# Softmax sums in a decoder layer: from matmuls of ones to exponentials of the row scores, and the transposed mask by a GpSimd selection

## The chip, the cores and the metric

One core of a Trainium2 chip runs one launch of the whole kernel. The metric is the device time of that launch in microseconds (us). The engines are TensorE (PE in the profile, its weight loads PEld), VectorE (DVE), ScalarE (ACT), GpSimd (POOL) and SyncE (SP). All five run their own instruction lists in order and wait for each other on semaphores.

## What is computed

Four batches of 512 tokens of width 512 pass through one decoder layer: attention with 16 heads of width 32 that share one key and one value head, a second block that is a quantised two-product network, and a gated feed-forward of width 1376 with low-rank experts. Only the attention is touched by the change.

```python
qkv = einsum('bsd,ed->bse', x, Wqkv_w) + Wqkv_b           # q: 16 heads x 32, k: 32, v: 32
scores = einsum('bqhd,bkd->bhqk', q, k) * HEAD_DIM ** -0.5
scores = where(tril(ones(S, S)), scores, finfo.min)
attn = softmax(scores, axis=-1)
ctx = einsum('bhqk,bkd->bqhd', attn, v)
out = einsum('bsd,ed->bse', ctx, out_w) + out_b
x = x + out                                              # of layernorm(x)
# then x = x + xattn(layernorm(x), ...), x = x + ffn(layernorm(x), ...)
```

## The kernel before

**Work.** Every engine's list is made from one list of steps, `ORDER`. It is merged from four streams: A (attention, `attention_steps`), L (layer norms and the quantised block, `layer_steps`), F (feed-forward, `feed_forward_steps`) and W (splitting the weights into a high and a low part, `preparation_steps`). Strings of the letters A, L, F and W (`FIRST`, `SECOND`, twice `STEADY`, `LAST`) say from which stream the next step is taken. Batches overlap: while batch b is in feed-forward, batch b+1 is in the quantised block and batch b+2 in attention. Batches 0 and 1 have no feed-forward beside their attention; batches 2 and 3 each have the whole feed-forward of an earlier batch beside theirs (110 of its gate and up pieces lie between the last `out` step of batch 1 and that of batch 2, and 110 more up to that of batch 3). After batch 3's attention only L and F are left.

**Attention.** A batch is done in four groups g of four heads. A group first needs the largest score of each query row. Step `max` (six per group, `MAX_GROUPS`; lines 1007 and 1011 on PE, 1295 on DVE) writes masked scores, rows = queries, into a PSUM slot, and DVE reduces them to `negm`, minus the largest score. Step `rows` turns `negm` with a PE transpose (L1018), splits it into high and low parts (ACT L800, DVE L1301), and two DMAs put them as extra rows under the queries in `qst`. Step `scores` (four per group, one for each tile kt of 128 keys; two halves each) writes transposed scores (rows = keys) less the row's largest score: two bf16 matmuls of `mask_bf` (L1029) put the mask into the diagonal tile, two matmuls (L1031) add the scores. ACT takes the exponential into `probs` (L811). Step `values` (L1045) multiplies `probs` with `v` into the PSUM tile `av` and with `ones` into the PSUM tile `den`, four heads side by side in four column groups of the array. Step `sums` copies `av` (DVE L1310) and `den` (ACT L818), step `context` takes the reciprocal of 128x512 sums in two halves (DVE L1315) and multiplies (DVE L1318), `split_context` splits the result (ACT L823, POOL L707), and `out` multiplies with the output weights.

**Buffers.** Two PSUM slots of two banks are shared by `turn1`, `kv`, `q`, `v`, `max`, `rows`, `scores`, `out` and the quantised block. A step claims the next of the two in turn (`Tenants.claim`), and PE waits there until the engine that read the slot last is done: for `max` that is DVE's reduction (`s_max`), for `scores` ACT's exponential (`p_ready`). The feed-forward and W use two other tiles, `ring`.

**Order on ACT.** ACT also does the tanh of each gate tile (L905), the split of `hd` (L909), and issues the DMA that loads the next `gu` tile.

## Time and profile before

| | |
|---|---|
| median of 3 runs | 1017.0 us (1016.59 to 1024.69) |
| profiled execution, its own time | 1015.68 us |
| its span | 1013.9 us |
| mean granted TensorE clock | 0.943 |
| PE busy | 923.5 us (91%) |
| DVE busy | 616.7 us (61%) |
| ACT busy | 313.1 us (31%) |
| POOL busy | 248.5 us (25%) |

Busy time of PE counts the pipelined latency of every matmul, so a busy PE can still be short of its rate. What one matmul takes from the next one is better read from the chain of work that ended last, where a piece runs only to the start of the next.

### The profile page before, as it was taken

The numbers are of one execution on the slowest core, as the hardware profiler recorded it, in microseconds if no ns is written. First come the engines' busy times: TensorE is split into PE (matmuls) and PEld (weight loads), VectorE is DVE, ScalarE is ACT, GpSimd is POOL, SyncE is SP. The second block draws the span as 40 slices with busy tenths as digits, with TensorE's granted clock in tenths as the row PEclk, the third lists the DMA queues.
The fourth block names the chain that finished last, engine by engine and source line by source line (L and its number), as shares of the span: only waits on it lengthen the run. The fifth ranks groups of instructions, "written<-read, shape, count | busy, mean of one in ns | idle before, by whom it ended". The sixth has DMA issues, their size and how long they took to land.

```text
span 1013.9 us, 13146 instructions
## 1 busy us (share of the span) xinstructions
PE 923.5 (91%) x5206; PEld 654.6 (65%) x5214; DVE 616.7 (61%) x865; ACT 313.1 (31%) x496; POOL 248.5 (25%) x217
## 2 busy tenths in 40 slices
PE   2898899587999999999999999999979999779997
PEld 1664456454457776667577776666757787568785
DVE  2345768778687687767565886765477565332222
ACT  2323442244353215342423135333222431121110
POOL 3612322421543022123210131231204033011110
PEclk9857979688799999999999999999999999999999
DMA  8963651832666843348344733354335455525442
GB/s 277 312 189 116 233 216 24 246 128 88 238 197 253 202 172 123 126 171 340 116 154 93 230 123 104 147 226 141 107 140 199 152 185 209 205 94 206 161 170 89
DMA packets 42913, 174.98 MB, mean 173 GB/s; under 512 B 5404, under 2 KB 8220, under 8 KB 32868
## 3 DMA queue, kind: packets, MB, share of 16 engines
q1 hardware_dynamic: 36804, 119.09, 34.7%
q10 hardware_dynamic: 6048, 55.05, 14.9%
q8 instruction: 42, 0.69, 0.3%
q14 instruction: 19, 0.16, 0.0%
HBM read 127.52 MB, written 33.75 MB: 159 GB/s over the span
## 4 chain that ended last, share of the span: by engine, by line
PE 74%; DVE 13%; issue 4%; DMA 3%; SPq 3%; ACT 2%; POOL 1%; POOLq 0%; DVEq 0%; ACTq 0%
PE ring L935 12%; PE ring L937 11%; PE ring L936 11%; PE av L1045 4%; PE slot L1031 4%; DVE negm L1295 4%; PE ring L1177 3%; PE den L1045 3%; PE slot L1011 3%; SPq L573 3%; PE slot L935 3%; PE slot L936 2%; PE slot L937 2%; PE slot L1114 2%; PE slot L1029 2%
## 5 line engine op out<-in xcount | busy, mean ns | idle before, releaser
L734 POOL TENSOR_TENSOR hd_l<-hd,hd_h 128x512 fp32r<-128x512 f32 x44 | 57.7, 1312 | 401.2 <-ACT hd_h L909 401.2
L935 PE MATMUL ring<-xT_h,gu 128*128 128x512 f32 x352 | 145.6, 414 | 5.0 <-DVE gated L1502 2.9
L936 PE MATMUL ring<-xT_l,gu 128*128 128x512 f32 x352 | 138.4, 393 | 0.0
L937 PE MATMUL ring<-xT_h,gu 128*128 128x512 f32 x352 | 138.3, 393 | 0.0
L1295 DVE TENSOR_REDUCE negm<-slot 128x4 f32<-128x512 f32 (+2 forms) x96 | 98.6, 1043 | 59.6 <-PE slot L1011 59.0
L811 ACT ACTIVATE probs<-slot 128x256 f32<-128x256 f32 (+3 forms) x128 | 85.0, 700 | 89.8 <-PE slot L1031 89.8
L935 PEld LDWEIGHTS ring<-xT_h,gu 128*128 128x128 f32 x352 | 66.8, 190 | 29.4 <-issue 11.5
L937 PEld LDWEIGHTS ring<-xT_h,gu 128*128 128x128 f32 x352 | 66.6, 189 | 14.9
L1541 DVE TENSOR_TENSOR total<-ring,total 128x512 f32<-128x512 f32 x64 | 44.0, 688 | 51.0 <-PE ring L937 50.9
L1031 PE MATMUL slot<-qst,kst 98*128 98x128 f32 (+3 forms) x256 | 74.8, 387 | 0.0
L936 PEld LDWEIGHTS ring<-xT_l,gu 128*128 128x128 f32 x352 | 67.0, 190 | 11.6
L1011 PE MATMUL slot<-kst,qst 96*128 96x128 f32 (+3 forms) x256 | 73.4, 397 | 0.0
L935 PE MATMUL ring<-dn,hd_h 128*128 128x512 f32 x176 | 70.1, 398 | 0.2 <-DVE ad_sum L1521 0.2
L937 PE MATMUL ring<-dn,hd_l 128*128 128x512 f32 x176 | 69.2, 393 | 0.0
L936 PE MATMUL ring<-dn,hd_h 128*128 128x512 f32 x176 | 69.1, 393 | 0.0
L909 ACT ACTIVATE hd_h<-hd 128x512 fp32r<-128x512 f32 x44 | 27.8, 631 | 119.1 <-DVE hd L1513 119.1
L905 ACT ACTIVATE gated<-ring 128x512 f32<-128x512 f32 x44 | 26.3, 599 | 122.5 <-PE ring L1177 122.3
L1513 DVE SCALAR_TENSOR_TENSOR hd<-gated,ring 128x512 f32<-128x512 f32 x44 | 30.2, 687 | 51.7 <-PE ring L1177 36.1
L1502 DVE SCALAR_TENSOR_TENSOR gated<-gated,ring 128x512 f32<-128x512 f32 x44 | 29.9, 680 | 50.5 <-ACT gated L905 50.5
L1315 DVE RECIPROCAL rden<-rden 128x256 f32<-128x256 f32 x32 | 55.8, 1744 | 0.1
L1029 PE MATMUL slot<-mask_bf 128*128 128x128 bf16 x256 | 38.8, 236 | 16.9 <-DVE negm L1295 7.7
L1045 PE MATMUL av<-probs,v 128*32 128x512 f32 (+3 forms) x512 | 52.3, 484 | 1.3 <-DVE cx L1310 1.1
(194 smaller groups left out, 1754.2 us busy)
## 6 DMA issues: line engine op xcount, KB each, us to landing
gu<-gu_parts ACTq DMA_DIRECT2D x42, 1280.0 KB, 5.5
dn<-dn_parts SPq DMA_DIRECT2D x12, 1728.0 KB, 7.7
gu_parts<-gu SPq DMA_DIRECT2D x11, 1280.0 KB, 5.7
qst<-qT_h SPq DMA_DIRECT2D x64, 128.0 KB, 2.4
raw_gu<-gu SPq DMA_DIRECT2D x11, 640.0 KB, 7.3
dn_parts<-dn SPq DMA_DIRECT2D x11, 576.0 KB, 7.7
dn<-dn_parts SPq DMA_DIRECT2D x4, 1152.0 KB, 5.1
x_in<-x SPq DMA_DIRECT2D x8, 512.0 KB, 4.8
```

Of the source, the lines that this page charges most:

```text
L734: pool.tensor_tensor(hd_l[:, i, :], hd[:, i, :], hd_h[:, i, :].bitcast(F32), ALU.subtract).then_inc(hd_lo.sem, 1)
L811: act.activation(probs[:, 2 * (step % 2) + pr, :, 0:n], slots[SLOT["scores", b, step, pr]][:, :, 0:n], ACT.Exp, scale=SCALE).then_inc(p_re ...
L935: pe.matmul(out_, w_hi_, m_hi_, start=start, stop=False, skip_group_check=True)
L936: pe.matmul(out_, w_hi_, m_lo_, start=False, stop=False, skip_group_check=True)
L937: return pe.matmul(out_, w_lo_, m_hi_, start=False, stop=stop, skip_group_check=True)
L1011: mm = pe.matmul(ps[:, bank, at * n:(at + 1) * n], qst[0:KROWS, 4 * g + h0 + h, qt * P:(qt + 1) * P], kst[0:KROWS, 0:n], start=False, stop ...
L1029: pe.matmul(ps[:, j, 0:P], mask_bf[:, 0, :], mask_bf[:, 2, :], start=True, stop=False, skip_group_check=True)
L1031: mm = pe.matmul(ps[:, j, 0:n], kst[0:KROWS + 2, kt * P:(kt + 1) * P], qst[0:KROWS + 2, 4 * g + 2 * pr + j, kt * P:T], start=False, stop=T ...
L1045: mm = pe.matmul(to[HD * c:HD * c + HD, kt * P:T], weights, probs[:, 2 * (step % 2) + c // 2, c % 2, 0:n], start=(kt == TT - 1), stop=(kt ...
L1295: dve.tensor_reduce(negm[:, h0:h0 + heads, qt].rearrange("p (a c) -> p a c", a=2), slots[SLOT["max", b, g, i]][:, :, 0:heads // 2 * n].rea ...
L1315: dve.reciprocal(rden[:, cols], rden[:, cols]).then_inc(rden_ready.sem, 1)
L1541: dve.tensor_tensor(total[:, tt, :], ring[RING["down", b, s, tt]][:, :], total[:, tt, :], ALU.add)\
```

## The change

The row sums no longer come from products with `ones`. Behind DVE's reduction of a `max` slot a new step `weigh` lets ACT take the exponential of each head's part of that slot (in place, bias = `negm`), with the sum along the row as a second output into `row_sum`. The slot is now free when these are done (`s_sum`). A new step `inverse` takes the reciprocal of 16 sums per row (DVE), which travel in the same transpose as the next group's `negm` (`rows`, five per batch instead of four), are split into high and low parts, and are spread over 32 rows per head by four matmuls (`spread`, with a loaded 0/1 matrix `spread_w`) into the PSUM tile `inv` in place of `den`. ACT copies it to `inv_sb`. `context` is one DVE multiplication of `av` in PSUM with `inv_sb`, per half. The mask of the transposed scores is no longer added by matmuls: POOL's `affine_select` sets the masked part of the diagonal tile of `probs` to zero behind ACT's exponential. A `scores` slot is free at the exponential (`p_exp`); `values` waits for the selection (`p_ready`). The scale 32^-0.5 moves from the exponential into the keys, with one more ACT copy of them. The `dn` tile has 3 slots instead of 4. The four strings of letters become one, `TURNS`, written out for all steps, with three `fill` steps (4, 1 and 4 spare matmuls of 256 columns).

```diff
@@ attention_steps
     for i in range(MG):
         yield ("max", b, 0, i)
+        yield ("weigh", b, 0, i)
...
-        yield ("scores", b, step)
+        yield ("scores", b, step, 0)
+        yield ("scores", b, step, 1)
...
-            for which in range(2):
-                yield ("values", b, step - 1, which)
+            yield ("values", b, step - 1)
         for key in maxima_among(g, idx):
             yield ("max", b, *key)
-        if idx == 0 and g:
-            yield ("sums", b, g - 1)
+            yield ("weigh", b, *key)
...
+        if idx == 3:
+            yield ("spread", b, g)
@@
-FIRST = (
...
+TURNS = (
+    "AAAAAAAAWAAAAWAAAAWWAAAAWAWAWAAWAAAAAAAAWAAAWAAAAAAAAAAWA4WAAAAWAAWWAAAAAWAAAAAAAWWAAAAAAAAAAAAAAAAAAAAAAAWAAA"
...
@@ gpsimd
+            def scores(b, step, pr):
+                diagonal = probs[:, 2 * (step % 2) + pr, :, 0:P]
+                pool.wait_ge(p_exp.sem, p_exp.at(b, 2 * step + pr + 1))
+                pool.affine_select(diagonal, diagonal, [[0, 2], [1, P]], ALU.is_ge, 0.0, base=0,
+                                   channel_multiplier=-1).then_inc(p_ready.sem, 1)
@@ scalar
+            def weigh(b, g, i):
+                qt, h0, heads = MAX_GROUPS[i]
+                n, per_bank = (qt + 1) * P, heads // 2
+                ps = slots[SLOT["max", b, g, i]]
+                act.wait_ge(s_max.sem, s_max.at(b, MG * g + i + 1))
+                for h in range(heads):
+                    part = ps[:, h // per_bank, h % per_bank * n:(h % per_bank + 1) * n]
+                    at = (h0 + h) * TT + qt
+                    ins = act.activation(part, part, ACT.Exp, bias=negm[:, g, at:at + 1], accum_out=row_sum[:, g, at:at + 1])
+                ins.then_inc(s_sum.sem, 1)
...
-                act.activation(rden[:, :], den[:, :], ACT.Copy).then_inc(den_out.sem, 1)
+                act.activation(inv_sb[:, :], inv[:, :], ACT.Copy).then_inc(inv_out.sem, 1)
@@ tensor
-                ps = in_slots.claim(pe, ("max", b, g, i), s_max, s_max.at(b, MG * g + i + 1))
+                ps = in_slots.claim(pe, ("max", b, g, i), s_sum, s_sum.at(b, MG * g + i + 1))
...
-                    for j in range(2):
-                        pe.matmul(ps[:, j, 0:P], mask_bf[:, 0, :], mask_bf[:, 2, :], start=True, stop=False, skip_group_check=True)
...
-                to, weights, read = ((av, v[:, kt, :], av_out), (den, ones[:, :], den_out))[which]
...
+            def spread(b, g):
+                pe.wait_ge(inv_lo.sem, inv_lo.at(b, g + 1))
...
+                for tt in range(TT):
+                    mm = pe.matmul(inv[:, tt * P:(tt + 1) * P], spread_w[:, tt, :], rows_hl[:, g, :], start=True, stop=True,
+                                   skip_group_check=True)
@@ vector
+            def inverse(b, g):
+                dve.wait_ge(s_sum.sem, s_sum.at(b, MG * g + MG))
+                dve.reciprocal(negm[:, g + 1, HD:HD + 4 * TT], row_sum[:, g, :]).then_inc(inv_ready.sem, 1)
...
-                dve.reciprocal(rden[:, cols], rden[:, cols]).then_inc(rden_ready.sem, 1)
...
-                dve.tensor_tensor(cx[:, g % 2, cols], cx[:, g % 2, cols], rden[:, cols], ALU.mult).then_inc(cx_ready.sem, 1)
+                dve.tensor_tensor(cx[:, g % 2, cols], av[:, cols], inv_sb[:, cols], ALU.mult).then_inc(cx_ready.sem, 1)
```

How this stands in the engines' lists. On PE, in batch 0's first group of heads, before (L1045 values and sums, L1018 the turn of `negm`, L1029 mask and L1031 scores):

```order
L1045 MATMUL av<-probs,v 32x128 x4
L1045 MATMUL den<-probs,ones 32x128 x4
L1018 MATMUL slot<-cst,negm 16x128
L1029 MATMUL slot<-mask_bf 128x128 x2
L1031 MATMUL slot<-qst,kst 128x384 x2
L1029 MATMUL slot<-mask_bf 128x128 x2
L1031 MATMUL slot<-qst,kst 128x384 x2
L1045 MATMUL av<-probs,v 32x256 x4
L1045 MATMUL den<-probs,ones 32x256 x4
```

The products with `ones` and the mask matmuls are gone, the turn is three times as wide, and pieces of W (`fold`, L997 and L1003) stand in between. The same place in the changed kernel (L1097 values, L1075 the turn, L1084 scores):

```order
L1097 MATMUL av<-probs,v 32x128 x4
L1075 MATMUL slot<-cst,negm 48x128
L997 MATMUL ring<-fold 128x128 x8
L1084 MATMUL slot<-qst,kst 128x384 x4
L1003 MATMUL ring<-fold 128x512
L1097 MATMUL av<-probs,v 32x256 x4
```

On ACT, from the first weight tile that is split in batch 0 up to the first exponentials, before:

```order
L767 ACTIVATE gu_102<-raw_gu_108 128x1280
L773 ACTIVATE dn<-raw_dn_110 128x576
L800 ACTIVATE negm_hl<-slot 16x128
L767 ACTIVATE gu_103<-raw_gu_109 128x1280
L811 ACTIVATE probs<-slot 128x2x128 x2
```

In the changed kernel the exponentials of the row scores (L835) stand between these, two or four behind each reduction:

```order
L835 ACTIVATE slot,row_sum<-slot,negm 128x128 x4
L799 ACTIVATE dn<-raw_dn_114 128x576
L835 ACTIVATE slot,row_sum<-slot,negm 128x256 x4
L793 ACTIVATE gu_107<-raw_gu_113 128x1280
L835 ACTIVATE slot,row_sum<-slot,negm 128x384 x2
L799 ACTIVATE dn<-raw_dn_115 128x576
L835 ACTIVATE slot,row_sum<-slot,negm 128x384 x2
L835 ACTIVATE slot,row_sum<-slot,negm 128x512 x4
L844 ACTIVATE rows_hl<-slot 16x128
```

Each of these now stands between the reduction and the next claim of that slot. On DVE, at the end of batch 0's attention, before:

```order
L1310 COPY cx<-av 128x512
L1315 RECIPROCAL rden<-rden 128x256
L1318 TENSOR_TENSOR cx<-cx,rden 128x256
L1315 RECIPROCAL rden<-rden 128x256
L1318 TENSOR_TENSOR cx<-cx,rden 128x256
```

The copy and the two wide reciprocals are gone there; a reciprocal of 16 columns and a split of the turned rows come in:

```order
L1360 RECIPROCAL negm<-row_sum 128x16
L1369 TENSOR_TENSOR rows_hl<-slot,rows_hl 16x128
L1380 TENSOR_TENSOR cx<-av,inv_sb 128x256 x2
```

In both orders the last `out` steps of the four batches have 0, 0, 110 and 220 gate and up pieces, and all 11 weight tiles of W by batch 1, ahead of them.

## Rows read from the trace of the kernel before

**Rows 1.** The page: span, granted clock in 40 slices (tenths), the reduction's group.

```profile
span 1013.9 us, 13146 instructions
...
PEclk9857979688799999999999999999999999999999
...
L1295 DVE TENSOR_REDUCE negm<-slot 128x4 f32<-128x512 f32 (+2 forms) x96 | 98.6, 1043 | 59.6 <-PE slot L1011 59.0
```

**Rows 2.** Six stretches: busy us (instructions) of five engines, granted clock, DMA.

```profile
0.00:41.00 41.00, 21.63 (x96) 16.30 (x96) 11.47 (x20) 14.27 (x23) 16.85 (x24) 1.00 0.88 296
41.00:152.00 111.00, 96.19 (x616) 56.30 (x617) 63.87 (x79) 38.21 (x59) 33.03 (x28) 0.75 0.58 198
152.00:312.00 160.00, 133.93 (x858) 84.42 (x859) 124.70 (x164) 62.84 (x96) 59.25 (x48) 0.84 0.50 162
312.00:524.00 212.00, 209.05 (x1246) 149.38 (x1247) 146.53 (x207) 70.34 (x114) 46.54 (x41) 1.00 0.51 177
524.00:737.00 213.00, 210.22 (x1254) 150.27 (x1255) 142.21 (x196) 70.92 (x115) 45.30 (x39) 1.00 0.44 151
737.00:1013.00 276.00, 252.49 (x1143) 197.90 (x1143) 127.93 (x202) 56.54 (x90) 47.55 (x38) 0.98 0.45 164
```

**Rows 3.** The residual addition behind `out`: the whole run, then 300 to 350 us.

```profile
L1323 DVE TENSOR_TENSOR x<-slot,x x8: 1208/1225/1226, 152.0 to 737.2; 128x1024 f32<-128x1024 f32 x8
...
L1323 DVE TENSOR_TENSOR x<-slot,x x2: 1208/1216/1225, 308.0 to 311.8; 128x1024 f32<-128x1024 f32 x2
```

**Rows 4.** The chain that ended last, shares of 41 to 312 us.

```profile
by line: DVE negm L1295 12.0%; PE av L1045 7.7%; PE slot L1011 6.6%; PE slot L1031 6.4%; PE den L1045 6.3%; DVE rden L1315 4.5%; PE ring L951 4.3%; PE ring L945 4.0%; issue 3.8%; PE slot L1007 3.6%; PE slot L1029 3.3%; SPq L573 3.1%; PE slo
```

**Rows 5.** The same chain, shares of 312 to 737 us.

```profile
by line: PE ring L935 14.9%; PE ring L937 13.4%; PE ring L936 13.3%; PE slot L1031 5.4%; PE av L1045 5.0%; PE den L1045 4.2%; PE ring L1177 3.8%; SPq L573 3.6%; PE slot L1011 3.5%; PE slot L937 3.4%; PE slot L935 3.4%; PE slot L936 3.4%; PE
```

**Rows 6.** Pieces of the chain, 485 to 500 us: start, us, what.

```profile
485.13 0.65 PE den L1045 x8
...
489.02 0.86 PE den L1045 x8
490.77 0.13 PE slot L1029 x2
...
491.97 0.22 PE den L1045 x8
...
497.25 0.43 PE den L1045 x8
```

**Rows 7.** Pieces of the chain, 640 to 652 us.

```profile
640.37 0.11 PE slot L1018
...
645.68 0.40 PE slot L1011 x4
```

**Rows 8.** ScalarE's groups by form: busy us, mean ns, idle before.

```profile
L811 ACT ACTIVATE probs<-slot 128x1024 f32<-128x1024 f32 x32 | 31.3, 1020 | 27.5 <-PE slot L1031 27.5
...
L811 ACT ACTIVATE probs<-slot 128x256 f32<-128x256 f32 x32 | 11.7, 383 | 19.2 <-PE slot L1031 19.2
L794 ACT ACTIVATE qT_h<-slot,bq_sb 128x512 fp32r<-128x512 f32 x16 | 11.0, 688 | 26.0 <-PE slot L937 25.7
...
L885 ACT ACTIVATE prob<-ring 128x32 f32<-128x32 f32 x4 | 0.8, 198 | 2.5 <-PE ring L1152 2.4
```

**Rows 9.** VectorE's wide reciprocals, by form.

```profile
L1315 DVE RECIPROCAL rden<-rden 128x256 f32<-128x256 f32 x32 | 55.8, 1744 | 0.1
```

**Rows 10.** The multiplication behind them: least, median and greatest ns.

```profile
L1318 DVE TENSOR_TENSOR cx<-cx,rden x32: 424/426/2857, 94.5 to 724.1; 128x256 f32<-128x256 f32 x32
```

**Rows 11.** GpSimd's groups by form nearest to a selection.

```profile
L707 POOL TENSOR_TENSOR hT_l<-cx,hT_h 128x256 fp32r<-128x256 f32 x32 | 25.3, 789 | 92.2 <-ACT hT_h L823 92.2
...
L644 POOL MEMSET kst<- 32x512 f32 x1 | 0.5, 520 | 0.1
```

**Rows 12.** TensorE's longest wait, 312 to 737 us: total, times, longest.

```profile
PE ring L935 <- DVE gated L1502: 2.9, 2, 1.6
```

**Rows 13.** Line 1045, what its engine stood idle for: us, times.

```profile
ACT probs L811: 8.8, 25
```

More of the change, by code:

```diff
@@ L143, in attention_steps @@
                 yield (("ln1_stats", "ln1_norm")[step - LN1_STEP], 1, h)
-    for which in range(2):
-        yield ("values", b, 15, which)
-    yield ("sums", b, 3)
+    yield ("values", b, 15)
     for hf in range(2):
@@ L287, in tenants_of @@
             slots.append(step)
-        elif name == "scores":
-            slots += [(*step, pr) for pr in range(2)]
         elif name == "prep_gu":
@@ L796, in rows_ @@
             def rows_(b, g):
+                ps = slots[SLOT["rows", b, g]]
                 act.wait_ge(m_ps.sem, m_ps.at(b, g + 1))
[L798 to L812 removed]
```

281 lines of the change are left out of this document (160 added, 121 removed).

## The prediction

> **What bounds the kernel now.** I read the busy times and clock by stretch first, then the chain of work that ended last in each, then the waits. The run falls into three parts, cut at the last residual addition of batches 1 and 3, at 312 and 737 us [rows 3]. From 312 to 737 us, where batches 2 and 3 have a feed-forward beside their attention, TensorE (PE) is busy 419 of 425 us at the full 2.4 GHz [rows 2], and its longest wait is 2.9 us in all [rows 12]: what PE is relieved of there comes back as time. From 41 to 312 us, the attention of batches 0 and 1, nothing is full: PE 230 and VectorE (DVE) 189 of 271 us, with a granted clock of 0.75 and 0.84 [rows 2]. The chain there changes between DVE's reductions (12.0%), PE and the reciprocals (4.5%) [rows 4], so this part is a latency problem, in which a longer way through a PSUM slot counts. After 737 us there is no attention, and the change doesn't reach it.
>
> **PE from 312 to 737 us.** This holds 8 groups of four heads. The products with ones take 0.22, 0.43, 0.65 and 0.86 us for the four key tiles [rows 6], 2.16 us a group, 17.3 us for 8; the chain's 4.2% of 425 us, 17.9, says the same [rows 5]. The mask takes 0.13 us for two matmuls [rows 6], 64 times, 8.3 us. Added are the spreading matmuls, four of 128 columns with 128-column weights a group, nearest to the four of 0.40 us in [rows 7]: 8 x 0.40 = 3.2 us; and one more turn a batch at 0.11 us [rows 7], 0.2 us. Net: -25.6 + 3.4 = **-22 us**. As 110 gate and up pieces stay in each of the two stretches, nothing fills the room but what was there. The cover that this needs: ScalarE (ACT), which is busy 141 of 425 us [rows 2], must do its new work beside PE.
>
> **What ACT gets.** An exponential costs 383 ns for 256 columns and 1020 for 1024, 0.83 ns a column; a 512-column activation with a per-row bias costs 688 ns [rows 8]. So the heads' parts of 128, 256, 384 and 512 columns cost 0.37, 0.48, 0.58 and 0.69 us, four of each a group: 8.5 us, or 1.41 us behind each of the six reductions, and 135 us in 16 groups. No row shows what the second output, the row sum, costs. Lower end nothing; upper end one further short instruction each, by the shortest ACT row 198 ns [rows 8], 51 us in 256. I take nothing, as it would be 0.2 us behind a head at most, and keep the 51 us for the range. On this the Trainium skill ("VectorE: DVE Perf Modes", Two Vector instructions with no wait between them) says that an operation which writes out its accumulator is two instructions. That is said of VectorE, and no row here shows it of ScalarE; if it held, 0.8 us more would stand behind a reduction of four heads, and it speaks against this change. The copy of `den` is replaced by a copy of the same size; a third key copy, about 0.7 us a batch, hides behind PE's query products.
>
> **41 to 312 us, removed.** From the chain: products with ones 6.3% of 271 us, 17.1 us; mask 3.3%, 8.9 us; reciprocals 4.5%, 12.2 us [rows 4]. In all DVE loses 55.8 us of reciprocals in the run [rows 9] for 16 tiny ones. The 26 us of PE I count in full, since PE is also what is late next there. Of the 12 us of DVE I count half: behind a reciprocal DVE has layer norms and weight folds waiting. Together -32 us.
>
> **41 to 312 us, added.** (1) The slot. The reductions hold 12.0% of the chain, 32.5 us, so with 1.04 us each [rows 1] 31 of the 48 lie on it. PE's part of such a slot is about 0.6 us (lines 1007 and 1011, 10.2% of 271 us [rows 4], over 48). Before, one slot could be filled while the other was reduced, and DVE set the pace, 1.04 us. Now a slot is held for 0.6 + 1.04 + 1.41 = 3.05 us, and two of them give 1.53 us: 0.49 us more, 31 times, 15 us. Ends: 0 if other steps always fill the gap, 44 us (31 x 1.41) if the exponentials are never overlapped. I take 15, because both slots exist and the interleaved steps are as many as before. Queued behind PE's wait for a slot are the scores and values of the group before; behind ACT's exponentials, the exponentials of `probs`. (2) The selection on GpSimd (POOL), 128 x (2 x 128), which no row shows. Nearest are 789 ns for a two-input operation on 128x256 and 520 ns for a memset of 512 columns, half of which is 260 [rows 11]; I take 0.5 us, one input and one output. PE stands behind an exponential at line 1045 only 25 times [rows 13]; 25 x 0.5 is 12 us, and as `values` comes after the next step's `scores`, I take a third, 4 us (ends 0 and 20). A gain isn't possible: it only adds to a way. POOL itself has room, 92 of 271 us busy plus 32 [rows 2]. (3) Spreading, 8 x 0.40 us, some at half clock: 4 us. (4) First batch: the load of the spread matrix, two bias and matrix copies: 1 us. Together +24, so **-8 us** net, from -38 to +35 by the ends.
>
> **Contention.** The multiplication of the context, two inputs in SBUF, is 426 ns in the median and 2857 at most [rows 10]; its new form reads `av` from PSUM. The Trainium skill ("GPSIMD Engine Reference", Key points) says that GpSimd shares its SBUF interfaces with VectorE, with contention on two SBUF inputs; the 2857 ns would be of that kind. It would make 128 more GpSimd instructions cost DVE something, and the new multiplication gain. I count neither.
>
> **Sum.** -22 - 8 = -30 us on the profiled 1015.7 us, which is 1.3 us below the median of 1017.0. Against the median: **987 us**. The nine spare matmuls, 3 slots of `dn` for 4, and the rewritten order count nothing: the former stand where PE waits, the middle one is touched by three stores.
>
> **Rivals.**
> *Slots and ACT's queue decide (slower), 1035 us.* In the full stretch the tanh of a gate tile stands in ACT's queue behind two to four exponentials (1.4 us or more), and `up`'s products cover it only for a short time: PE already waits 2.9 us for `gated` [rows 12]. Half a us more on each of 22 column tiles is 11 us; a third of the 48 maxima finding its slot 1.41 us late is 22 us. That makes -22 + 33 = +11 there. With 30 us instead of 15 for the slot, the latency part is at -8 + 15 = +7: 1017 + 18 = 1035. It decides from the point where ACT's way through a slot is longer than what PE has between two claims of it. For it: PE runs in order and has just two slots. Against: ACT is a third busy there. 10%.
> *Nothing net in the latency part, or lost again, 1003 us.* The slot costs 23 us or more; only the -22 stays, with some of it given back. 15%.
> *A colder clock, 1001 us.* The clock of 0.75 and 0.84 means 56 and 51 us at 1.2 GHz [rows 2]. PE is given less to do between the same waits, and may hold the low level for longer. 50 us more of it, with PE on half of the chain, is 50 x 0.5 x 0.5 = 13 us. The Trainium skill ("TensorE: Matmul & The Clock Gate", Why this matters for your kernels) says that gaps without PE work bring the half clock back. The page of the profile shows the low slices just where PE has gaps [rows 1]. 5%.
> *No change, 1012 us.* The mask and the ones turn out to have been cover for waits (transfers of `gu` among them), and the full stretch gives only half. 10%.
> *All of it, 966 us.* The exponentials hide, and the 38 us come back whole: -22 - 38 + 9. 18%.
>
> **Numbers.** The forecast, 975 to 1000, has 42%. A measurement of this kernel tells about 1% from no change, 1007 to 1027 us. Faster by more: 42 + 18 + 15 + 5, less a little of the 1003 case that passes 1007, 0.78; same 0.12; slower 0.10. The range of 8 in 10 leaves out the slower case, the upper part of no change and the lowest of the best case: 958 to 1014.
>
> **What the next profile would show.** Right: no matmuls with ones, PE busy down by some 80 us in its pipelined count, ACT up to about 450 us, 312-to-737's counterpart near 403 us with PE still above 97% busy; first two batches 41 to about 304. Row sums: a second ACT instruction behind each exponential, or none. Wrong: PE waits at line 1058 for `s_sum` or at a gate for `gated` of more than 10 us in the stretch of batches 2 and 3; a selection of over 1 us; a mean clock under 0.93.

## The result

The changed kernel takes **1040.2 us** in the median (1038.06 to 1043.18, four runs), and the kernel before, run beside it, 1020.3 us (1016.59 to 1024.69). The ratio is 1.0207, 95% interval 1.0173 to 1.0242: about 2% slower, where 987 us, 3% faster, was forecast. The time lies above the forecast's range. Medians are of all runs, ratios of the fast runs alone, which leaves out one slow run each in two of the experiments.

The page of the changed kernel, first its span, then the granted clock in 40 slices, then the reduction's group, the one of [rows 1]:

```profile
span 1041.4 us, 12384 instructions
...
PEclk9855558755668999999999999999998999989999
...
L1354 DVE TENSOR_REDUCE negm<-slot 128x4 f32<-128x512 f32 (+2 forms) x96 | 100.3, 1045 | 91.4 <-PE slot L1062 91.0
```

The middle four of the six stretches of [rows 2] have these counterparts. Columns are the stretch, its length, busy us (instructions) of PE, PEld, DVE, ACT and POOL, granted clock, DMA share and GB/s:

```profile
41.00:174.00 133.00, 116.50 (x474) 70.11 (x475) 49.48 (x76) 72.98 (x191) 49.10 (x63) 0.56 0.54 184
174.00:354.00 180.00, 144.10 (x695) 91.95 (x696) 115.02 (x173) 99.91 (x232) 68.58 (x77) 0.69 0.44 149
354.00:554.00 200.00, 193.49 (x1040) 142.32 (x1041) 125.55 (x188) 104.02 (x243) 60.84 (x73) 0.99 0.51 178
554.00:767.00 213.00, 201.93 (x1086) 149.22 (x1087) 132.16 (x196) 106.81 (x250) 58.98 (x71) 0.99 0.46 156
```

They are cut at the last residual addition of each batch, as before [rows 3]. Those of the changed kernel start at 173.8, 353.5, 553.9 and 766.2 us. So, counted from 41 us, batches 0 and 1 take 312.5 us instead of 270.8, **41.7 more**, batches 2 and 3 412.7 instead of 425.4, **12.7 less**, and the rest 275.2 instead of 276.7. The clock fell in the first two from 0.75 and 0.84 [rows 2] to 0.56 and 0.69: 229 of 312 us at 1.2 GHz, where it had been 106 of 271.

Such stretch figures come from one profiled run of each kernel. That of the changed kernel took 1043.2 us, 3.0 above its median, and that of the kernel before 1015.7, 4.6 below the median beside it, at one of its highest clocks (0.943, where its runs beside the experiments had 0.926 to 0.943). So 7.6 of the 27.5 us between the two profiles are scatter. In batches 0 and 1, where the clock varies, I take differences under some 5 us as not shown; in batches 2 and 3 the figures repeat within 1 us among the kernels that hardly differ there (412.7, 412.3 and 412.1 us).

One correction to this cut. The new order does one batch's routing and low-rank entry earlier, ahead of batch 1's last `out`. TensorE's groups of the changed kernel, 41 to 354 us (busy us, mean ns), hold it; in those of the kernel before, 41 to 312 us, these products don't occur:

```profile
L1205 PE MATMUL ring<-xT_h,route_hl 128*16 128x512 f32 x4 | 1.6, 395 | 0.0
L1206 PE MATMUL ring<-xT_l,route_hl 128*8 128x512 f32 x4 | 1.6, 393 | 0.0
L987 PE MATMUL ring<-xT_h,gaua_h 128*128 128x512 f32 x4 | 1.6, 393 | 0.0
L988 PE MATMUL ring<-xT_l,gaua_h 128*128 128x512 f32 x4 | 1.6, 390 | 0.0
L989 PE MATMUL ring<-xT_h,gaua_l 128*128 128x512 f32 x4 | 1.6, 390 | 0.0
L1214 PE MATMUL ring<-tail_c,lT 16*128 16x8 f32 x8 | 1.1, 254 | 0.0
```

That is 9.1 us of busy time moved, not lost. If each of them counts as a microsecond of the run in both places, batches 0 and 1 lose 32.6 us and batches 2 and 3 gain **3.6**, where -8 and -22 were forecast. (In batches 2 and 3 TensorE is busy nearly all the time, so there this holds; in batches 0 and 1 it is an upper bound.)

ScalarE's groups by form. The new exponentials take 127.6 us in all, and behind each stands a second instruction that reads the row sum out:

```profile
L835 ACT ACTIVATION_READ_ACCUMULATOR slot<-slot,negm 128x1 f32 x256 | 51.4, 201 | 0.0
L835 ACT ACTIVATE slot<-slot,negm 128x512 f32<-128x512 f32 x64 | 42.0, 657 | 21.4 <-DVE negm L1354 21.4
L835 ACT ACTIVATE slot<-slot,negm 128x384 f32<-128x384 f32 x64 | 35.3, 552 | 31.9 <-DVE negm L1354 31.8
...
L835 ACT ACTIVATE slot<-slot,negm 128x256 f32<-128x256 f32 x64 | 28.6, 447 | 11.0 <-DVE negm L1354 10.9
...
L835 ACT ACTIVATE slot<-slot,negm 128x128 f32<-128x128 f32 x64 | 21.7, 339 | 39.5 <-DVE negm L1354 39.5
```

What TensorE waited for in batches 0 and 1 (us, times, longest), then in batches 2 and 3. The waits behind L835 are those of its slots:

```profile
PE slot L1084 <- ACT slot L835: 14.2, 13, 2.0
PE slot L1058 <- ACT slot L835: 13.5, 12, 2.3
PE slot L1058 <- DMA qst<-qT_h: 8.2, 2, 4.2
PE slot L1084 <- DVE rows_hl L1369: 5.2, 5, 3.8
...
PE slot L1075 <- ACT slot L835: 2.2, 1, 2.2
...
PE slot L1140 <- ACT slot L835: 1.6, 1, 1.6
```

```profile
PE ring L987 <- DMA gu<-gu_parts: 6.3, 3, 3.9
PE slot L1058 <- issue: 3.4, 2, 2.1
PE ring L987 <- DVE y_u L1592: 2.1, 2, 1.1
```

In the first two batches 31.5 us in 27 waits stand behind the exponentials. Before, 22 waits there stood behind the reductions alone, 16.7 us. The waits are less than half of the loss: in the profiles TensorE's idle time grew there from 41 us (270.8 less 230.0 busy) to 52 (312.5 less 260.1), and its busy time, with fewer products to do, from 230 to 260 us, 9 of them the moved routing. In batches 2 and 3 no wait at all stands behind the exponentials. The waits for `gu` have grown there from 1.0 us to 6.3; [rows 12] had 2.9 us, for `gated`, as the longest, and no such wait is left.

### The profile page after: what moved, and what is told of

Same layout as the page of the kernel before. It is cut to its first block, busy times and chain, and to the rows that moved or that the text cites. A ratio compares the mean times of both kernels' runs of the same rounds, so it can differ in the third digit from the quotient of the medians.

```text
span 1041.4 us, 12384 instructions
## 1 busy us (share of the span) xinstructions
PE 928.3 (89%) x4515; PEld 666.5 (64%) x4523; DVE 559.5 (54%) x849; ACT 455.2 (44%) x1030; POOL 301.9 (29%) x346
## 3 DMA queue, kind: packets, MB, share of 16 engines
q10 hardware_dynamic: 6048, 55.05, 14.9%
## 4 chain that ended last, share of the span: by engine, by line
PE 73%; DVE 9%; ACT 5%; issue 5%; DMA 4%; POOL 2%; SPq 1%; POOLq 0%; DVEq 0%; ACTq 0%
PE ring L987 11%; PE ring L988 10%; PE ring L989 10%; PE slot L1084 5%; PE av L1097 5%; PE slot L1062 4%; PE ring L1239 4%; DMA gu<-gu_parts 3%; PE slot L987 3%; PE slot L989 3%; PE slot L988 3%; PE ring L997 2%; ACT slot L835 2%; DVE negm L1354 2%; PE slot L1176 2%
## 5 line engine op out<-in xcount | busy, mean ns | idle before, releaser
L835 ACT ACTIVATE slot<-slot,negm 128x128 f32<-128x128 f32 (+3 forms) x256 | 127.6, 499 | 103.8 <-DVE negm L1354 103.5
L1354 DVE TENSOR_REDUCE negm<-slot 128x4 f32<-128x512 f32 (+2 forms) x96 | 100.3, 1045 | 91.4 <-PE slot L1062 91.0
L862 ACT ACTIVATE probs<-slot 128x256 f32<-128x256 f32 (+3 forms) x128 | 87.5, 703 | 57.4 <-PE slot L1084 56.3
L727 POOL TENSOR_SCALAR_AFFINE_SELECT probs<-probs 128x256 f32<-128x256 f32 x128 | 59.8, 474 | 159.9 <-ACT probs L862 159.2
L1084 PE MATMUL slot<-qst,kst 98*128 98x128 f32 (+3 forms) x256 | 79.8, 415 | 21.0 <-ACT slot L835 14.2
L1062 PE MATMUL slot<-kst,qst 96*128 96x128 f32 (+3 forms) x256 | 83.2, 438 | 0.0
L1084 PEld LDWEIGHTS slot<-qst,kst 98*128 98x128 f32 x256 | 52.8, 239 | 46.2 <-ACT slot L835 21.2
L1058 PE MATMUL slot<-mask_bf 128*128 128x128 bf16 (+1 forms) x192 | 38.0, 290 | 25.9 <-ACT slot L835 13.5
```

Of the source, the lines that this page charges most:

```text
L727: pool.affine_select(diagonal, diagonal, [[0, 2], [1, P]], ALU.is_ge, 0.0, base=0, channel_multiplier=-1).then_inc(p_ready.sem, 1)
L835: ins = act.activation(part, part, ACT.Exp, bias=negm[:, g, at:at + 1], accum_out=row_sum[:, g, at:at + 1])
L862: act.activation(probs[:, 2 * (step % 2) + pr, :, 0:n], slots[SLOT["scores", b, step, pr]][:, :, 0:n], ACT.Exp)\
L1062: mm = pe.matmul(ps[:, bank, at * n:(at + 1) * n], qst[0:KROWS, 4 * g + h0 + h, qt * P:(qt + 1) * P], kst[0:KROWS, 0:n], start=False, stop ...
L1084: mm = pe.matmul(ps[:, j, 0:n], kst[0:KROWS + 2, kt * P:(kt + 1) * P], qst[0:KROWS + 2, 4 * g + 2 * pr + j, kt * P:T], start=True, stop=Tr ...
L1354: dve.tensor_reduce(negm[:, g, 0:4 * TT].rearrange("p (h q) -> p h q", q=TT)[:, h0:h0 + heads, qt].rearrange("p (a c) -> p a c", a=2), slo ...
```

## The experiments

Each was timed beside the kernel before; "stretch" figures are batches 0 and 1, then batches 2 and 3, of the profiled run, against 270.8 and 425.4 us of the kernel before and 312.5 and 412.7 us of the changed one. Cold is the time at 1.2 GHz within batches 0 and 1 (106 us before, 229 after).

**The products put back.** First the mask as a product (here with no effect on the scores, as it is overwritten):

```diff
+                    pe.matmul(ps[:, j, 0:P], mask_bf[:, 0, :], mask_bf[:, 1, :], start=True, stop=True, skip_group_check=True)
                 for j in range(2):
```

> The changed kernel with the 256 bf16 mask products back on TensorE, two ahead of each half of a scores step, overwritten by the scores (the result is unchanged). Clock theory (the products taken away had kept TensorE above what it needs for 2.4 GHz): the time at 1.2 GHz in the first two batches, 229 us of 41 to 354 us, falls by 40 us or more and the run is at 1030 us or less although 8 us of work are added in each half of the run. Slot theory (the exponentials in the max slots make the loss): the clock hardly moves and the run is 8 to 17 us longer than the changed kernel, 1048 to 1057 us.

Measured: 1047.3 us, 1.0274 (1.0225 to 1.0323); stretches 313.2 and 417.2. The products cost nothing in the first two batches and 4.5 us in the full ones. Cold fell from 229 to 201 us, less than the clock theory asked, and brought no time.

Then also four products a step in place of those with `ones`, into `inv`:

```diff
+                if 4 * b + g + (kt == 0):
+                    pe.wait_ge(inv_out.sem, 4 * b + g + (kt == 0))
+                for c in range(4):
+                    mm = pe.matmul(inv[HD * c:HD * c + HD, kt * P:T], v[:, kt, :], probs[...], start=True, stop=True, ...)
                 mm.then_inc(pv_done.sem, 1)
```

> The changed kernel with the mask products and the second set of products with probs back (into the inv tile, overwritten by the spreading products), so that TensorE has the same work as in the kernel before plus spreading. Clock theory: time at 1.2 GHz near the 106 us of the kernel before, run at 1020 to 1030 us. Slot theory: batches 2 and 3 give back their 12 us and more, nothing is gained ahead of them, run at 1065 to 1085 us.

Measured: 1076.4 us, 1.0566 (1.0514 to 1.0617); stretches 328.5 and 431.6. All the products are worth 36 us, 18.9 of them in the full stretch and 16.0 in batches 0 and 1. So they do cost something there, a third of the 47.8 us that they kept TensorE busy in the kernel before; with them cold falls from 229 to 198 us. The wait that comes with them, for ScalarE's copy of `inv`, held nothing up: TensorE's matmuls never stood behind it, a weight load once for 0.6 us.

**The exponentials of the row scores left out**, one short ScalarE instruction behind each reduction in their place:

```diff
-                for h in range(heads):
-                    ...
-                    ins = act.activation(part, part, ACT.Exp, bias=negm[:, g, at:at + 1], accum_out=row_sum[:, g, at:at + 1])
+                ins = act.activation(row_sum[...][:, heads_of, qt], negm[...][:, heads_of, qt], ACT.Exp, scale=0.0)
                 ins.then_inc(s_sum.sem, 1)
```

> The changed kernel without the exponentials of the row scores: one short ScalarE instruction per max step writes ones in place of the sums, so the softmax is not normalised. Slot theory: the max slots are free 1.2 to 2.2 us earlier, 48 times in the first two batches, run at 1000 us or less, and TensorE's waits for ScalarE at max and scores slots (27.7 us) go. Clock theory alone: the waits go, but the clock stays at 0.5 to 0.6 in the first two batches, run at 1020 to 1035 us.

Measured: 1013.8 us, 0.9941 (0.991 to 0.9972); stretches 285.1 and 411.3. The exponentials cost 26 us by the medians; by stretches 27.4 us in batches 0 and 1, where cold falls to 177 us without them, and 1.4 in batches 2 and 3. The run isn't at the 1000 us or less of the slot theory. Without the exponentials (41 to 326 us), then with them (41 to 354 us), columns as in the stretches above:

```profile
41.00:326.00 285.00, 247.35 (x1167) 155.78 (x1169) 162.00 (x249) 113.75 (x217) 119.37 (x141) 0.69 0.53 182
...
41.00:354.00 313.00, 260.60 (x1166) 162.06 (x1169) 164.49 (x248) 172.89 (x423) 117.69 (x140) 0.63 0.48 164
```

So of the 28 us that lie between these two lines about 15 are idle time of TensorE (52.4 for 37.7), and 13 are products that take longer. In batches 2 and 3 TensorE waits as before for `gu`, and so not because of the exponentials:

```profile
PE ring L986 <- DMA gu<-gu_parts: 8.0, 3, 3.7
PE slot L1057 <- issue: 3.4, 2, 2.1
PE ring L986 <- DVE y_u L1591: 2.1, 2, 1.0
```

**The order of the kernel before**, with all else as changed:

```diff
-TURNS = (...)
+FIRST = (...)   # the four strings and the attention steps of before;
+                # weigh behind its max, both score halves together, spread and inverse behind their step
```

> The changed kernel with the order of the kernel before: its letters, each old attention step replaced by the new steps up to its counterpart, no spare matmuls. Order theory (the rewritten order makes the loss): 1005 to 1020 us. Slot and clock theory: within 10 us of the changed kernel's 1040 us, since the work and the slots are the same.

Measured: 1071.0 us, 1.0505 (1.0453 to 1.0558); stretches 319.6 and 430.8. The new order gains 31 us. In the old one TensorE stands 15 us behind the exponentials in batches 2 and 3, and never for `gu`.

**Spare products for the clock**: two more of 256 columns ahead of each `max` and `scores` in batches 0 and 1, with the exponentials and without them.

```diff
             for name, *where in ORDER:
+                if name in ("max", "scores") and where[0] < 2:
+                    fill(2)
```

> The changed kernel with two spare bf16 products of 256 columns on TensorE ahead of each max and scores step of batches 0 and 1 (112 places, 24 us of work at 2.4 GHz, 48 us at 1.2 GHz), written to the free ring tile, where they run while TensorE would wait for a slot. Clock theory (the time at 1.2 GHz, 229 us of 41 to 354, costs some 40 us there): the time at 1.2 GHz falls by more than 80 us and the run is at 1030 us or less despite the added work. Slot theory alone: the spare products are only work, 1050 to 1070 us.

> The same spare products in the kernel without the row exponentials (1014 us; its softmax is not normalised). Clock theory: time at 1.2 GHz from 177 us to under 100 us, run at 1000 us or less. Otherwise 1020 to 1035 us.

Measured: 1039.3 us, 1.0193 (1.0166 to 1.0221), stretches 305.0 and 417.0; and 1018.1 us, 0.9981 (0.9954 to 1.0007), stretches 284.1 and 409.9. Cold falls from 229 us to 150, and without the exponentials from 177 to 119; the clock of the page, with both exponentials and spare products, is now

```profile
PEclk9856889757679989999999999999999999899999
```

and the time stays, or with the exponentials left out grows by 4 us, the intervals overlapping (1040.2 and 1013.8 us without the spare products). What the clock gives, the spare work takes.

**The kernel before without the removed products**, all else as it was: neither mask nor `ones` products (but for one group), so masking and sums are left out:

```diff
-                    for j in range(2):
-                        pe.matmul(ps[:, j, 0:P], mask_bf[:, 0, :], mask_bf[:, 2, :], ...)
...
-                for c in range(4):
+                for c in range(4) if which == 0 or b + g == 0 else ():
```

> The kernel before, in its own order, without the mask products and, but for the first group of heads, without the products with ones (the mask and the sums are wrong); ScalarE and VectorE do all that they did. It asks what TensorE's relief is worth alone. If all of it comes back: 1020 - 26 (batches 2 and 3) - 25 (batches 0 and 1) = 967 to 975 us. If the clock takes the part of batches 0 and 1 back, 990 to 1000 us with more than 140 us at 1.2 GHz ahead of 312 us.

Measured: 997.2 us, 0.9752 (0.9697 to 0.9808); stretches 271.7 and 401.2. This is the experiment that decides on my sum. In the full stretch the products are worth 24.2 us (25.6 forecast). In batches 0 and 1 the profiles show nothing for them, and the interval (20 to 31 us in all) leaves at most some 7 us outside of batches 2 and 3; 26 had been counted. TensorE's groups of the same products there, in this kernel,

```profile
L1029 PE MATMUL slot<-qst,kst 98*128 98x128 f32 (+3 forms) x128 | 46.7, 479 | 18.7 <-DVE negm L1293 8.1 <-DVE negm_hl L1299 6.7 <-ACT probs L811 1.5
L1011 PE MATMUL slot<-kst,qst 96*128 96x128 f32 (+3 forms) x128 | 44.9, 470 | 0.0
L1043 PE MATMUL av<-probs,v 128*32 128x128 f32 (+3 forms) x256 | 33.8, 615 | 1.8 <-DVE cx L1308 1.7
L945 PE MATMUL ring<-fold 8*128 8x128 f32 x160 | 23.8, 359 | 0.0
...
L951 PE MATMUL ring<-fold 8*128 8x512 f32 x22 | 18.3, 923 | 0.6 <-DVE raw_gu L1230 0.6
```

in the kernel before, 41 to 312 us, with the removed `den` and mask (L1029) among them,

```profile
L1011 PE MATMUL slot<-kst,qst 96*128 96x128 f32 (+3 forms) x128 | 41.8, 444 | 0.0
L1031 PE MATMUL slot<-qst,kst 98*128 98x128 f32 (+3 forms) x128 | 41.6, 417 | 0.0
L1045 PE MATMUL av<-probs,v 128*32 128x128 f32 (+3 forms) x256 | 28.5, 525 | 1.3 <-DVE cx L1310 1.1
L1045 PE MATMUL den<-probs,ones 128*32 128x128 f32 (+3 forms) x256 | 27.3, 504 | 0.0
L1029 PE MATMUL slot<-mask_bf 128*128 128x128 bf16 x128 | 20.5, 248 | 16.9 <-DVE negm L1295 7.7 <-DVE negm_hl L1301 6.9 <-DVE hid L1436 1.1
L945 PE MATMUL ring<-fold 8*128 8x128 f32 x160 | 20.0, 314 | 0.0
...
L951 PE MATMUL ring<-fold 8*128 8x512 f32 x22 | 16.3, 828 | 0.5 <-DVE raw_gu L1232 0.5
```

and in the changed kernel:

```profile
L1062 PE MATMUL slot<-kst,qst 96*128 96x128 f32 (+3 forms) x128 | 50.7, 521 | 0.0
L1084 PE MATMUL slot<-qst,kst 98*128 98x128 f32 (+3 forms) x128 | 49.8, 505 | 20.5 <-ACT slot L835 14.2 <-DVE rows_hl L1369 5.2 <-DVE hid L1498 1.1
L1097 PE MATMUL av<-probs,v 128*32 128x128 f32 (+3 forms) x256 | 35.5, 643 | 0.0
L997 PE MATMUL ring<-fold 8*128 8x128 f32 x160 | 28.2, 406 | 0.0
...
L1003 PE MATMUL ring<-fold 8*128 8x512 f32 x22 | 21.8, 1091 | 0.0
```

The same five groups (scores, maxima, `av` and the two of the weight folds) take 148.2 us before, 167.5 without the removed products and 186.0 in the changed kernel. 47.8 us of busy time go (27.3 `den`, 20.5 mask), and the rest grows, by 19.3 us in the one and 37.8 in the other, since more of it runs at 1.2 GHz (160 us and 229, for 106).

**The selection left out** (the diagonal tiles stay unmasked):

```diff
-                pool.affine_select(diagonal, diagonal, [[0, 2], [1, P]], ALU.is_ge, 0.0, ...).then_inc(p_ready.sem, 1)
...
-                pe.wait_ge(p_ready.sem, ...)
+                pe.wait_ge(p_exp.sem, ...)
```

> The changed kernel without the GpSimd selection: values wait for the exponential itself, the mask of the transposed scores is missing. If the selection lies on the way, as VectorE and TensorE never wait for it by name (1.8 us of waits), 1035 to 1040 us; if it costs what the prediction had counted, 4 us, 1036; if the selection carries the loss, 1025 us or less.

Measured: 1040.3 us, 1.0195 (1.0142 to 1.0247); stretches 311.9 and 412.1. It costs nothing. Its duration in the changed kernel, least, median and greatest:

```profile
L727 POOL TENSOR_SCALAR_AFFINE_SELECT probs<-probs x128: 398/409/1397, 72.8 to 748.9; 128x256 f32<-128x256 f32 x128
```

**The exponentials alone, added to the kernel before** (sums still from `ones`, order as before):

```diff
+            def weigh(b, g, i): ...      # as in the change
-                ps = in_slots.claim(pe, ("max", b, g, i), s_max, ...)
+                ps = in_slots.claim(pe, ("max", b, g, i), s_sum, ...)
```

> The kernel before, in its own order, with the row exponentials and their sums added behind every reduction and the max slots held until they are done (the sums are not used; all products stay). Slot theory: the first two batches take some 27 us longer as between the changed kernel and its form without exponentials, or more, since this order was not laid out for it: 1045 to 1075 us. If the exponentials cost only beside the freed products, 1020 to 1030 us.

Measured: 1090.8 us, 1.0703 (1.0665 to 1.0742); stretches 325.1 and 444.6: 54.3 and 19.2 us more. TensorE waited 48.8 us behind them in batches 0 and 1, and 14.9 in 2 and 3, by all its waits at a slot.

**The way of the sums left out as well as the exponentials**: no `inverse`, no wide turn, no `spread`; the context is multiplied by 0.5.

```diff
-                dve.tensor_tensor(cx[:, g % 2, cols], av[:, cols], inv_sb[:, cols], ALU.mult)
+                dve.tensor_scalar(cx[:, g % 2, cols], av[:, cols], 0.5, None, ALU.mult)
```

> The changed kernel without the row exponentials and without all that carries the sums (reciprocal, the wider turn, its two splits, spreading products, copy of inv; the context is multiplied by 0.5, the softmax is not normalised). Left of the change: fewer products, selection, the new order. If the way of the sums adds waits of its own (rows of the next group wait for the sums of this one), the first two batches fall from 285 us to 270 or less and the run is at 995 us or less. If only the clock and the order matter there, 1008 to 1014 us.

Measured: 1008.9 us, 0.9888 (0.986 to 0.9916): 5 us less than with it; stretches 288.8 and 406.1. The gain lies in batches 2 and 3 (5.2 us), and the first two are far from the 270 us that waits of this way's own would have given back.

**The selection alone, in the kernel before.** Only the mask products go, sums and order stay:

```diff
-                        pe.matmul(ps[:, j, 0:P], mask_bf[:, 0, :], mask_bf[:, 2, :], ...)
...
+            def scores(b, step):
+                for pr in range(2):
+                    ...
+                    pool.affine_select(diagonal, diagonal, [[0, 2], [1, P]], ALU.is_ge, 0.0, ...)
```

> The kernel before, in its own order, with only the second part of the change: the mask by GpSimd's selection in place of 256 mask products. If batches 2 and 3 give back the 8 us of their 64 pairs of products and the clock takes the rest: 1010 to 1014 us. If the selection is late in this order: 1020 or more.

Measured: **1007.9 us**, 0.9885 (0.9853 to 0.9918), computing everything. This half of the change beats both kernels. Its first two batches take 273.4 us, 2.6 more than before, which the scatter covers. Its full stretch (two stretches at 314 to 522 and 522 to 729 us) is 414.2 us long, 11.2 less than before, and TensorE is still busy 409.7 us of it:

```profile
314.00:522.00 208.00, 204.52 (x1190) 148.74 (x1189) 146.53 (x207) 69.90 (x114) 58.58 (x73) 1.00 0.51 180
522.00:729.00 207.00, 205.19 (x1198) 149.57 (x1197) 142.29 (x197) 70.52 (x116) 57.06 (x71) 1.00 0.46 156
```

Without the exponentials the changed kernel still lost 14 us in batches 0 and 1. Four more runs went to that.

**The order of before, without the exponentials** (the edits of the third and the fourth experiment together):

> The changed kernel in the order of steps of the kernel before, and with one small ScalarE instruction behind each reduction in place of the exponentials of the row scores: the row sums are wrong, since the exponentials and their sums are left out. Without the exponentials the changed kernel took 14 us more for batches 0 and 1 than the kernel before, and 14 us less for batches 2 and 3. Theory A (the new order, drawn up for slots that are held long, costs those 14 us where they are not): batches 0 and 1 near 272 us, batches 2 and 3 402 to 412, in all 990 to 1000 us. Theory B (the order helps here as it did with the exponentials, by 31 us; the 14 us are the way of the sums and the selection): batches 0 and 1 285 to 295 us, batches 2 and 3 at 415 to 430, in all 1020 to 1040 us.

Measured: 1010.5 us, 0.9905 (0.9878 to 0.9932); stretches 280.8 and 410.8. Neither theory holds. The order changes nothing in the sum that the intervals can tell (1013.8 against 1010.5), and up to 9.1 of the 14 us are the routing that the new order moves forward. That put back, the new order without the exponentials has 276.0 and 420.4 us, 4.8 less and 9.6 more than the old one. With the exponentials it was worth 31 us.

**The exponentials without their sums**, one short instruction a reduction in place of two to four readings:

```diff
-                    ins = act.activation(part, part, ACT.Exp, bias=..., accum_out=row_sum[:, g, at:at + 1])
+                    act.activation(part, part, ACT.Exp, bias=...)
+                ins = act.activation(row_sum[...], negm[...], ACT.Exp, scale=0.0)
```

> The changed kernel, its exponentials of the row scores without the sum as second output, and one small ScalarE instruction behind each reduction's exponentials: the row sums are left out and wrong. So 256 second instructions of 201 ns (51 us) go from ScalarE, up to 0.8 us behind a reduction, and 96 small ones of about 0.2 us come in. Leaving out exponentials and sums together gave 26 us. Theory A (every 0.1 us in the way of a slot counts alike in the first two batches): the second instructions are 51 of the 179 us, less the 19 us of small ones that the kernel without exponentials has too; 7 to 10 us of the 26 come back, 1030 to 1034 us. Theory B (only the exponentials' length decides, the second instruction hides behind the waits between heads): 1038 to 1041 us. Theory C (the rate of the slots is a threshold and this takes most of it away): 1020 to 1026 us.

Measured: 1040.5 us, 1.022 (1.0186 to 1.0254), the same as with them. The 51.4 us of second instructions, less 20.4 of the short ones, cost no time that the medians show. Its profiled run, 4 us faster than its median, has stretches of 302.5 and 412.3 us, 10 us less in batches 0 and 1 than that of the changed kernel, which was 3 us slower than its own; what is left of the 10 is within the scatter.

**No ScalarE instruction at all behind a reduction**, the slot free at the reduction:

```diff
-                ps = in_slots.claim(pe, ("max", b, g, i), s_sum, ...)
+                ps = in_slots.claim(pe, ("max", b, g, i), s_max, ...)
-                dve.reciprocal(negm[:, g + 1, HD:HD + 4 * TT], row_sum[:, g, :])
+                dve.reciprocal(negm[:, g + 1, HD:HD + 4 * TT], negm[:, g, 0:4 * TT])
```

> The changed kernel without any ScalarE instruction behind a reduction: a max slot is free at the reduction, as before, and the reciprocal takes the largest scores instead of the row sums, so exponentials and row sums are left out and the output is wrong. The kernel with one short ScalarE instruction in their place took 1013.8 us, 285 us of it for batches 0 and 1, against 271 us before. Theory A (the way through a third engine is what is left of the loss): batches 0 and 1 at 268 to 276 us, in all 998 to 1004 us. Theory B (the order, the way of the sums or the clock hold the 14 us): 281 to 288 us there, in all 1009 to 1015 us.

Measured: 1014.9 us, 0.9974 (0.9944 to 1.0004), stretches 287.6 and 409.1: no better than with the short instruction (1013.8). Theory A falls for the changed kernel.

**The short instruction alone, in the kernel before:**

> The kernel before, with one short ScalarE instruction (0.2 us, of 2 or 4 columns) behind each of the 96 reductions, at which alone the slot is free; nothing is left out. Theory A (the way through a third engine costs by itself): 48 such ways in batches 0 and 1, 31 of them on the path by the chain, at 0.3 to 0.4 us each, 9 to 15 us; some 5 us more in batches 2 and 3; in all 1030 to 1040 us. Theory B (only a long hold costs; the second slot covers a short one): 1018 to 1024 us.

Measured: 1031.2 us, 1.0109 (1.0067 to 1.0152); stretches 280.5 and 426.4. The instruction lasts 0.21 us, and TensorE waits for it, 41 to 321 us:

```profile
PE slot L1039 <- ACT row_sum L803: 11.2, 18, 1.2
...
PE slot L1017 <- ACT row_sum L803: 6.1, 7, 2.1
```

So the bare way through a third engine costs 12 us in the order of before, by the profiles 9.7 in batches 0 and 1, and nothing in the new order. Its 17.3 us of waits stand where 16.7 stood behind the reductions, so most of the 9.7 isn't waiting: TensorE is idle 1 us longer and busy 9 us longer, with 129 us cold for 106. Why the new order bears it was not tried further.

The runs make a ladder. Its last line has the 9.1 us of moved routing put back into batches 2 and 3:

| kernel | median, us | batches 0 and 1 | batches 2 and 3 |
|---|---|---|---|
| before | 1020 | 270.8 | 425.4 |
| without the removed products | 997.2 | 271.7 | 401.2 |
| with the way of the sums, the selection and the short instruction, old order | 1010.5 | 280.8 | 410.8 |
| with the exponentials, old order | 1071.0 | 319.6 | 430.8 |
| changed kernel: new order | 1040.2 | 303.4 | 421.8 |

## Why the prediction was wrong

*Batches 2 and 3, -22 forecast, -3.6 measured once the moved routing is counted.* The price of the products was right: 24.2 us where they alone go. I had set against it 3.4 us, for spreading and one turn. By the ladder three things stand against it: the new carrying of the sums with the selection and the short instruction, 9.6 us (by the runs in the new order 5.2 us of it is the way of the sums, and the selection nothing); the new order itself, 9.6 us without the exponentials; and the exponentials, 1.4 us. Of the added matmuls, the turn took 0.22 us (0.11 forecast) and the four spreading matmuls 0.40 to 0.59 (0.40), by these pieces of the chain of the changed kernel (start, us, what):

```profile
511.08 0.22 PE slot L1075
...
519.78 0.59 PE inv L1108 x4
...
536.19 0.40 PE inv L1108 x4
```

So two terms failed here: "3.4" for what is added, and the rewritten order, set among those that "count nothing". "The cover that this needs: ScalarE must do its new work beside PE" did hold in the changed kernel, with 1.4 us and no wait behind L835. But it held by the order, which the prediction did not count: in the old one the exponentials cost 20.0 us there (410.8 to 430.8), where the slower rival had put 33. In the new order the same place holds waits for `gu`, waits whose cause the profile doesn't show (issue), and waits for `y_u`, 11.8 us against the 5.1 us of the three longest before. They stand there without the exponentials too (13.5 us) and not in the old order, so it is the order that brings them, and not the three slots of `dn`, which the runs in the old order have too. Which of its steps does is not separated.

*Batches 0 and 1, -8 forecast, +32.6 measured.* By the ladder: 0.9 us for the removed products (-26 forecast), 9.1 for the way of the sums with the selection and the short instruction (9 forecast, less 6 for the reciprocals), 38.8 for the exponentials (15), and 16.2 back by the new order (0). Two steps failed, and they are of different kinds.

First, the removed work: "The 26 us of PE I count in full, since PE is also what is late next there." In the kernel before it was worth nothing that the profiles show, 271.7 us against 270.8, and 7 us at most. (Put back into the changed kernel, the same products cost 16.0 us there, still less than the 26; why they are worth more there was not tried.) I took shares of the chain as if the remaining pieces kept their duration. They don't: with fewer products between the same waits TensorE stood at 1.2 GHz for 160 us instead of 106, and five groups of the others grew by 19.3 us, so that its busy time stayed at 229 us for 230. By an estimate from these numbers, 54 us more at half the clock take back up to 27 us of work, about as much as was removed. The rival "a colder clock" named this at 13 us and 5%. The Trainium skill ("TensorE: Matmul & The Clock Gate", Why this matters for your kernels) says that gaps without PE work bring the half clock back, and this trace agrees: the granted clock of the changed kernel is 0.56 and 0.69 where TensorE is idle 52 of 312 us, and 0.99 where it is idle 18 of 413. As the products alone go, the clock of 41 to 312 us falls from 0.80 to 0.70.

Second, the slot term, 15 us, "because both slots exist and the interleaved steps are as many as before". It measured 27.4 us in the new order and 38.8 in the old one (280.8 to 319.6). By the waits 31.5 us stood behind L835. The exponentials themselves were priced right, 0.37 to 0.69 us against 339 to 657 ns. My formula, two slots that fill each other's time, gives 0.49 us for each of 31 reductions; the measured 27.4 over 48 is 0.57 us, over the 31 on the chain 0.88. The hold was longer than I had put, 1.86 us of ScalarE a reduction (127.6 + 51.4 us over 96) for 1.41, and with it the formula gives 22 us; but the run without the readings does not bear that out. The other half of the cost the formula does not know at all: 13 of the 28 us are TensorE's longer busy time, at a clock of 0.63 for 0.69. So the term was mis-sized, not misplaced, and lies within the ends of 0 and 44.

*The row sum's second output, taken as nothing.* There is a second instruction, of 201 ns, 51.4 us in all. The passage of the Trainium skill ("VectorE: DVE Perf Modes", Two Vector instructions with no wait between them) that I had set beside it, and that speaks of VectorE, describes what ScalarE does in this trace. But it costs no time that the medians show: leaving it out gave 1040.5 us. The upper end had the engine's time right and the run's wrong, and this is not the cause of the miss.

*The selection, 4 us, and its 0.5 us.* 409 ns in the median, 474 in the mean, no time at all in the run (1040.3 us without it). Weight loads waited for it 1.8 us in all, as the `values` behind it come after the next step's scores.

*Reciprocals, half of 12 us.* No run took them away alone. The kernel with neither exponentials nor way of the sums has none, and needs 288.8 us in batches 0 and 1, 279.7 without the moved work; the one that keeps them without the products needs 271.7. But the first of these has the new order as well, so what the reciprocals were worth is not shown.

*A sum of the prediction.* Its own ends give -33 to +37 us for batches 0 and 1, with half the reciprocals at the upper one, and not -38 to +35. The measured +32.6 lies inside of either; the run left its range because both parts came out on the slow side.

*What the next profile would show.* PE's busy time was to fall by 80 us and is 928.3 us, 4.8 more than before: the products are gone, and what is left takes longer. The mean clock is 0.879, under the 0.93 that I had named as a sign of error. In batches 2 and 3 PE is busy 395 of 413 us, 96% where more than 97 was named. ACT's 455.2 us are as forecast (450), and the waits behind `s_sum` or `gated` in batches 2 and 3, the first sign of error, did not come.

*The rewritten order "counts nothing".* With the exponentials it was worth 31 us of gain, without them nothing. Of the rivals, "slots and ACT's queue decide", 1035 us at 10%, came nearest in its time, but by luck: it put +11 us into batches 2 and 3 and +7 into batches 0 and 1, where -3.6 and +32.6 were measured, and no wait for `gated` was left that its queue of the tanh needs. Its slot held for long is what the waits behind L835 show, in batches 0 and 1.

What stays open: the traces divide the cost of the exponentials in batches 0 and 1 into about 15 us of idle time and 13 of longer products, but whether the clock falls because of those waits, and what would be left of the loss at a full clock, no run separates. The spare products raise the clock and shorten the waits behind L835 (31.5 to 23.7 us), but add their own work. Open too is which steps of the new order make it bear the exponentials and cost 9.6 us in batches 2 and 3.

## What to carry to other kernels

A product that goes from a stretch where its engine is full comes back as time, 24 of 25.6 us here; from a stretch where that engine waits and its clock already falls, it can come back as little or nothing (nothing that the profiles show in the kernel before, 16 us for 47.8 of busy time in the changed one). Before moving a sum from TensorE to a third engine, look at what that engine's instructions hold: 1.9 us of exponentials and readings behind a reduction, on one of two slots, cost 60 us in one order of steps and 26 in another. Split a change of two halves and time each: the selection in place of the mask products alone gave 1.1%, and the other half took back more than that.

## What the runs showed of the hardware

An exponential with a row sum on ScalarE is two instructions, 339 to 657 ns for 128 to 512 columns and then 201 ns for the reading, and the second could be left out without a gain in the median. From 41 to 174 us TensorE had a granted clock of 0.56, while the profile calls it busy for 116.5 of 133 us; before, it was 0.75 with 96.19 of 111 us busy [rows 2]. At a like busy share, 0.88 and 0.87, the clock differed; the same products of the weight fold took 406 ns for 314 in the mean over 41 to 354 and 41 to 312 us, so slow products also count as busy. `affine_select` on 128x256 took 409 ns in the median (398 to 1397), less than a two-input operation of that shape (789 ns [rows 11]). The multiplication of the context with one input in PSUM took 415 to 426 ns in all 32 cases, where the one with both in SBUF had reached 2857 ns [rows 10]:

```profile
L1380 DVE TENSOR_TENSOR cx<-av,inv_sb x32: 415/415/426, 110.7 to 754.5; 128x256 f32<-128x256 f32 x32
```
